# A graph layer and an expert layer on one core: statistics of the nodes with three reciprocal roots, and another order of bias transfers, turns and the last sum

## The reference, cut to what matters

```
x [6250, 256] f32; src, dst [100000] int32 (edges sorted by dst)
def mlp(h): return relu(h @ w1 + b1) @ w2 + b2

xn   = layernorm(x)
msgs = mlp(xn[dst])                          # one message an edge
agg  = segment_sum(msgs, src, 6250)          # summed by source node
x    = x + mlp(xn + agg)

f = layernorm(x)                             # one "batch" of 6250 tokens
w = softmax(softmax(mean(f) @ Wr + br) * capacity scale); top 2 of 8 experts
y = sum over the 2 experts: w_e * (gelu(f @ W1[e] + b1[e]) @ W2[e] + b2[e])
out = x + layernorm(y + f) * gamma + beta
```

## Time and profile before

| | before |
|---|---|
| runs | 1018.24, 1019.18 (median), 1019.61 us |
| profiled execution | 1018.42 us |
| its span, first to last instruction | 1016.6 us |
| busy: PE, DVE, POOL, ACT | 91%, 77%, 60%, 56% |
| granted TensorE clock, mean | 0.964 |

### The profile page before, as it was taken

One profiled execution on the slowest core, in us unless ns is written; L12 is line 12 of the kernel. 1 busy time (PEld: TensorE's weight loads), 2 busy tenths in 40 slices (PEclk: granted clock), 3 DMA queues, 4 the chain that ended last, 5 costly groups with the idle time before them and its releaser, 6 DMA issues.

```text
span 1016.6 us, 15925 instructions
## 1 busy us (share of the span) xinstructions
PE 925.1 (91%) x5067; PEld 549.2 (54%) x5067; DVE 784.3 (77%) x2245; ACT 569.3 (56%) x1143; POOL 609.9 (60%) x635
## 2 busy tenths in 40 slices
PE   5899994869999999899999999999489999999996
PEld 2455552334555555555555555555256666766675
DVE  7889993986776776866876876865668788889995
ACT  6899962435355354455454455454278677566661
POOL 2102114767777777777777777777005667666774
PEclk8899897999999999999999999999769999999999
DMA  9853899333433443434334434333120000000001
GB/s 302 118 100 99 143 143 306 109 84 97 139 102 105 112 122 101 113 104 133 102 98 115 121 98 125 105 98 105 27 94 6 22 22 22 33 32 21 22 22 63
DMA packets 61740, 98.66 MB, mean 97 GB/s; under 512 B 9014, under 2 KB 47399, under 8 KB 61655
## 3 DMA queue, kind: packets, MB, share of 16 engines
q0 software_dynamic: 26640, 61.37, 25.1%
q1 hardware_dynamic: 34426, 35.31, 10.9%
q10 hardware_dynamic: 588, 0.93, 0.3%
HBM read 77.79 MB, written 19.78 MB: 96 GB/s over the span
## 4 chain that ended last, share of the span: by engine, by line
PE 66%; DVE 14%; ACT 8%; issue 4%; DMA 4%; POOL 3%; SPq 0%; DVEq 0%; ACTq 0%; POOLq 0%
PE bank L1325 23%; PE bank L1473 12%; PE bank L1459 11%; PE bank L1315 6%; PE bank L1306 6%; PE bank L1345 3%; DMA zb_table<-G 2%; POOL G L799 2%; PE bank L1200 2%; DVE G L1908 1%; PE bank L1215 1%; ACT XT L950 1%; PE bank L1355 1%; DVE G L1906 1%; ACT G L992 1%
## 5 line engine op out<-in xcount | busy, mean ns | idle before, releaser
L865 POOL DMA_INDIRECT G<-table,edge_row x355 | 354.6, 999 | 113.9 <-issue 107.2
L1325 PE MATMUL bank<-G,MHL 128*128 128x512 f16 x1372 | 353.0, 380 | 0.2 <-DVE XT L1937 0.2
L1010 ACT ACTIVATE G<-bank 128x512 f16<-128x512 f32 x343 | 203.8, 597 | 215.5 <-PE bank L1315 214.6
L1325 PEld LDWEIGHTS bank<-G,MHL 128*128 128x128 f16 x1372 | 132.6, 97 | 96.0 <-issue 1.6
L1315 PE MATMUL bank<-G 128*128 128x256 f16 x686 | 135.1, 278 | 12.7 <-DVE G L1908 12.5
L1908 DVE TENSOR_TENSOR G<-iota_two,in_cell 128x512 f16<-128x512 f16 x343 | 144.1, 420 | 0.0
L1906 DVE TENSOR_TENSOR G<-iota_two,in_cell 128x256 f16<-128x256 f16 x343 | 99.6, 290 | 43.9 <-PE bank L1315 19.0
L1473 PE MATMUL bank<-MHL 128*128 128x256 f16 (+1 forms) x1176 | 130.6, 273 | 0.4 <-DVE G L2179 0.3
L1473 PEld LDWEIGHTS bank<-MHL 128*128 128x128 f16 (+1 forms) x1176 | 115.2, 98 | 16.6 <-DVE MHL L2023 0.7
L1315 PEld LDWEIGHTS bank<-G 128*128 128x128 f16 x686 | 66.1, 98 | 95.6 <-DVE G L1908 20.2
L1459 PE MATMUL bank<-G,MHL 128*128 128x512 f16 x528 | 115.9, 379 | 1.9 <-ACT G L1082 1.9
(11 more groups left out here) (345 smaller groups left out, 1234.1 us busy)
## 6 DMA issues: line engine op xcount, KB each, us to landing
X<-in_L_gnn_b POOLq DMA_DIRECT2D x12, 512.0 KB, 12.9
zb_table<-G SPq DMA_DIRECT2D x12, 512.0 KB, 4.7
table<-MHL SPq DMA_DIRECT2D x12, 512.0 KB, 6.2
XT<-zb_table SPq DMA_DIRECT2D x12, 512.0 KB, 3.9
G<-table,edge_row POOLq DMA_INDIRECT x355
out<-G SPq DMA_DIRECT2D x11, 512.0 KB, 2.9
X<-in_x SPq DMA_DIRECT2D x2, 1536.0 KB, 14.8
X<-in_x SPq DMA_DIRECT2D x2, 1024.0 KB, 10.6
```

What stands on the lines that cost most here:

```text
L865: e.indirect_dma_start(rows[g % RING][:, j, :], None, table, bass.IndirectOffsetOnAxis(ap=edge_row[:, at:at + 1], axis=0),).then_inc(s_row ...
L1010: e.activation(blocks[c % ARING].rearrange("p a b -> p (a b)")[:, 0:n], bank[3 + c % 2][:, 0:n], ACT.Copy).then_inc(s_ev, 1)
L1325: ins = e.matmul(bank[1 + m][:, :], MHL[:, t, h * D + m * P:h * D + (m + 1) * P], blocks[c % ARING].rearrange("p a b -> p (a b)"), start=( ...
```

## The change

There are six parts.

1. **Statistics.** The batches of tiles are cut a little otherwise, and the reciprocal roots are taken apart from them: `scale_tiles(j)` makes one root for each range of `STAT_ROOTS`, three in all instead of six. The first two batches stand ahead of the keys, the next behind the first sorting stage with the bounds, and the last behind the second stage.
2. **Jobs in the sort.** `copy_low(0)` to `copy_low(9)` stood ahead of stages 8, 13, 17, 20, 24, 30, 35, 42, 48 and 53 and stand now behind stages 2, 6, 11, 15, 17, 23, 29, 35, 41 and 47. `copy_low(10)`, which stood behind the sort, stands behind stage 54 of 55. TensorE's three small jobs go one step later.
3. **First nodes.** `transposes(0)` goes ahead of the second product of the bound, and ACT counts 1 and then, behind `copy_turned(0)`, 3 instead of 4 at once.
4. **Bias transfers.** POOL issues eight of them ahead of the run list instead of five, and the run list and the load of `run_first` then directly one after the other.
5. **The tail.** `root_slot` and `turn_slot` replace the fixed distances for the last items: tiles 24, 25 are turned in slot 133 instead of 131, tiles 26, 27 in slot 136 instead of 132; tile 47 gets its root in slot 136 instead of 132 and its turn in 138 instead of 134. The one-hots of the last sum are made one slot sooner, ahead of the roots of tiles 24 to 27.
6. **ACT's copy of a round** stands at the head of its slot instead of at its end.

```diff
 Y_BANKS = 3
-STAT_BATCHES = [(0, 4), (4, 8), (8, 16), (16, 28), (28, 40), (40, TILES)]
+STAT_BATCHES = [(0, 4), (4, 8), (8, 16), (16, 28), (28, 38), (38, TILES)]
+STAT_ROOTS = [(0, 8), (8, 16), (16, TILES)]
 STAT_MOST = max(z - a for a, z in STAT_BATCHES)
...
         SLOTS_ALL = items[-1][0] + TURN_AFTER + 1
+        LAST_SUM = PRE + 2 * (GROUPS * ROUNDS - 1)
         ITEM_TILES = [len(tiles) for _, tiles in items]
...
+        def root_slot(s):
+            t, tiles = items[s]
+            return LAST_SUM + 3 if tiles[0] == TILES - 2 else t + ROOT_AFTER
+        def turn_slot(s):
+            t, tiles = items[s]
+            if tiles[0] == TILES - 2:
+                return LAST_SUM + 5
+            at = t + TURN_AFTER
+            if at == LAST_SUM - 1:
+                return LAST_SUM + 3
+            return LAST_SUM if at == LAST_SUM - 2 else at
+        def turns_due(k):
+            return [(s, tiles) for s, (_, tiles) in enumerate(items) if turn_slot(s) == k]
         def roots_due(k):
             out = []
-            for s, tiles in due(k, ROOT_AFTER):
+            for s, tiles in ((s, tiles) for s, (_, tiles) in enumerate(items) if root_slot(s) == k):
                 if tiles[0] >= FIRST:
...
-            for q in range(5):
+            for q in range(8):
                 add_b2(q)
             e.wait_ge(s_run_at, 2)
             e.dma_start(run_list.rearrange("(p t) -> p t", t=A_STRIDE), runs_t[0:n_class, :]).then_inc(s_run_list, 16)
-            add_b2(5)
             e.wait_ge(s_run_list, 16)
             e.indirect_dma_start(run_first[0:CLASS_ROWS, :], None, run_list.rearrange("(r t) -> r t", t=1),
                                  bass.IndirectOffsetOnAxis(ap=class_run[0:CLASS_ROWS, 0:1], axis=0)).then_inc(s_run_first, 16)
-            for q in range(6, STEPS):
+            for q in range(8, STEPS):
                 add_b2(q)
...
                 for i, t in enumerate(tiles_of(q)):
-                    e.wait_ge(s_stat, 1 + sum(t >= z for _, z in STAT_BATCHES))
+                    e.wait_ge(s_stat, 1 + sum(t >= z for _, z in STAT_ROOTS))
                     e.activation(xn_in[q % 2][:, i, :], X[:, t, :], ACT.Identity, bias=nmr[:, t:t + 1],
...
                              bias=abs_b1[:, m:m + 1], scale=LNORM_MAX).then_inc(s_hbc, 1)
-            count_more(4)
+            count_more(1)
...
             copy_turned(0)
+            count_more(3)
             normalise(1)
...
                 copy_blocks([c + 2 for c in chunks_of(k) if c + 2 < CHUNKS])
-                for s, tiles in due(k, TURN_AFTER):
+                for r in round_due(k, 0):
+                    if r == 0:
+                        e.wait_ge(s_keep, 1)
+                    e.wait_ge(s_agg, GROUPS * (r + 1))
+                    since(e, s_tu, max(r - 1, 0))
+                    e.activation(U[r % 2][:, :], bank[0][:, 0:D], ACT.Copy, scale=keep[:, 0:1]).then_inc(s_uh, 1)
+                for s, tiles in turns_due(k):
                     e.wait_ge(s_tx, s + 1)
...
                         e.activation(h, h, ACT.Relu).then_inc(s_hd, 1)
-                for r in round_due(k, 0):
-                    if r == 0:
-                        e.wait_ge(s_keep, 1)
-                    e.wait_ge(s_agg, GROUPS * (r + 1))
-                    since(e, s_tu, max(r - 1, 0))
-                    e.activation(U[r % 2][:, :], bank[0][:, 0:D], ACT.Copy, scale=keep[:, 0:1]).then_inc(s_uh, 1)
             e.wait_ge(s_dif, 1)
...
             ins.then_inc(s_hb, 1)
-            e.wait_ge(s_hbc, KD)
-            for k in range(KD):
-                e.matmul(bank[7][0:1, 0:D], hidden_bound[:, k:k + 1], abs_w[1][:, k, :], start=(k == 0), stop=False)
-            e.matmul(bank[7][0:1, 0:D], ones[0:1, 0:1], abs_b2[0:1, :], start=False, stop=True).then_inc(s_hb, 1)
-
             def transposes(q):
...
                     ins.then_inc(s_tp, 1)
+            transposes(0)
+            e.wait_ge(s_hbc, KD)
+            for k in range(KD):
+                e.matmul(bank[7][0:1, 0:D], hidden_bound[:, k:k + 1], abs_w[1][:, k, :], start=(k == 0), stop=False)
+            e.matmul(bank[7][0:1, 0:D], ones[0:1, 0:1], abs_b2[0:1, :], start=False, stop=True).then_inc(s_hb, 1)
...
-            transposes(0)
             e.wait_ge(s_scale, 1)
             e.matmul(bank[7][:, 0:2], ones[0:1, :], bound[0:1, 2:4], start=True, stop=True).then_inc(s_scp, 1)
             for q in range(STEPS):
                 hidden(q)
                 if q + 1 < STEPS:
                     transposes(q + 1)
-                if q == 3:
+                if q == 4:
                     rank_rows()
-                elif q == 4:
+                elif q == 5:
                     sum_runs()
-                elif q == 5:
+                elif q == 6:
                     turn_runs()
...
                     multiply(c)
-                for s, tiles in due(k, TURN_AFTER):
+                for s, tiles in turns_due(k):
                     turn_x(s, tiles)
...
                     step(e.bn_aggr(mv2[:, t, :], stat_in[:, t - a, :]))
+            def scale_tiles(j):
+                a, z = STAT_ROOTS[j]
                 settle()
...
-            aux = {1: [(statistics, 1), (scale_bounds,), (statistics, 2)], 6: [(statistics, 3)], 7: [(copy_low, 0)],
-                   11: [(row_tiles,)], 12: [(copy_low, 1)], 14: [(class_numbers,)],
-                   16: [(class_counts,), (copy_low, 2), (select_rows,)], 18: [(class_runs,)],
-                   19: [(statistics, 4), (copy_low, 3)], 23: [(copy_low, 4)], 25: [(class_rows_of,)], 28: [(statistics, 5)],
-                   29: [(copy_low, 5)], 34: [(copy_low, 6), (run_starts,)], 41: [(copy_low, 7)],
-                   47: [(copy_low, 8), (place_rows,)], 52: [(copy_low, 9)]}
+            aux = {1: [(statistics, 2), (scale_bounds,), (scale_tiles, 1), (statistics, 3), (statistics, 4)],
+                   2: [(statistics, 5), (scale_tiles, 2), (copy_low, 0)], 6: [(copy_low, 1), (row_tiles,)],
+                   11: [(copy_low, 2)], 14: [(class_numbers,)], 15: [(copy_low, 3)],
+                   16: [(class_counts,), (select_rows,)], 17: [(copy_low, 4)], 18: [(class_runs,)],
+                   23: [(copy_low, 5)], 25: [(class_rows_of,)], 29: [(copy_low, 6)],
+                   34: [(run_starts,)], 35: [(copy_low, 7)], 41: [(copy_low, 8)],
+                   47: [(copy_low, 9), (place_rows,)], 54: [(copy_low, 10)]}
             s_, d_ = src_in[0:EDGE_ROWS, :], dst_in[0:EDGE_ROWS, :]
...
             statistics(0)
+            statistics(1)
+            scale_tiles(0)
             e.wait_ge(s_dst, 16 * len(EDGE_PARTS))
...
             sum_flags()
-            copy_low(10)
             copy_low(11)
...
-                if slot(k)[0] == "gather":
+                if slot(k)[0] == "gather" and k < LAST_SUM:
                     one_hots(*slot(k)[1:])
...
                 prepare(k + 2)
+                if k + 3 == LAST_SUM:
+                    one_hots(*slot(k + 3)[1:])
                 if k + 2 < BATCHES:
```

## The result

| | before | changed |
|---|---|---|
| median of 20 runs each | 1019.09 us | 1016.14 us |
| lowest and highest | 1016.72, 1021.70 us | 1013.06, 1019.09 us |
| ratio, 95% interval | | 0.9972 (0.9963 to 0.9980) |
| span of the profiled execution | 1016.6 us | 1014.3 us |
| busy: PE, DVE, POOL, ACT | 91%, 77%, 60%, 56% | 91%, 77%, 60%, 56% |

By the ratio the changed kernel is 0.28% faster, 2.9 us. The forecast was 4.0 us faster, 1015.2 us.

A forecast was written before the change was run, and what follows sets the result against it. TensorE's products were taken as the bound except in the sorting phase and the tail of the sums. -1.4 (sorting) - 2.6 (tail) = -4.0 us on 1018.42 gave 1014.4, forecast as 1015.2 for the median; range 1010.5 to 1020.5.

The forecast's parts named there:

- The start, +1.5: Start of the sorting phase: statistics moved ahead make `scale_bounds`, and ACT's loop with it, 1.5 us later.
- Rival 2: Sorting phase: the sort is not late, as TensorE's clock rises earlier or ACT gains; 2.6 us more, 1012.6; chance 0.12.
- The end of the sort, 157.2: Sorting phase: early low-half copies wait for ACT, so the key list goes out at 157.2 instead of 149.24 us.
- The relief: Sorting phase: bias additions end before the sort does, so ACT's 2.35 and 6.60 us store waits go and later landings shrink.
- the mark: End of the sorting phase, when POOL may issue the third class batch: 179.3 instead of 180.71 us, a gain of 1.4.
- rival 1: After the sort: landings stay as long while the sort ends later, 1024.6 us; chance 0.25 including a half relief.
- The tail, -2.6: Last sums: one-hots ahead of the root and tile 47's root behind DVE's addition bring that addition 2.6 us sooner.
- The middle, 0: Middle phase: ACT's copy leading its slot for each round was costed at nothing.
- Rival 4: Sorting phase: TensorE falls to 1.2 GHz once more, costing ACT one to three us, 1017; chance 0.13 together with another rival.

The follow-up runs named there:

- third run of the changed kernel: The changed kernel with nothing further edited, timed again against the kernel before on one chip: 1015.96 against 1022.54 us, ratio 0.9936.

## Why the prediction was right, and where not

**The start, +1.5.** Right: `scale_bounds` came 1.49 us later (25.18 to 26.67). ACT's loop ran 1.2 us later in the trace of the result (its first copy into `G` at 36.23 instead of 35.05), because TensorE's first hidden products, which begin at 28.49 instead of 27.03, took 6.06 us instead of 6.35: they began 1.5 us later, and the granted clock rose less than that later (0.68 and 0.90 in 32 to 34), so fewer of them ran at 1.2 GHz. How much that gives differs from trace to trace. In the third run of the changed kernel the same products took 5.08 us, and ACT's copy began at 35.36, only 0.4 us later than with bias order and tail (34.97, on another chip). Rival 2 named this; it gave 0.3 us in one trace and more than a microsecond in the other.

**The end of the sort, 157.2.** Right: 156.70, with `copy_low(8)` at 132.99 (133.4 forecast) and `copy_low(10)` in time. DVE waits for ACT's high copies as forecast.

**The relief, and the mark 179.3.** The mark is 179.28. Its terms: key list at 156.70 (forecast 157.2), 3.92 to the first windows (4.6), 15.77 to the merge (14.6), 2.89 to the batch (2.9). That the mark is met to the tenth is luck: the first two terms were 1.2 us too long together, and the third, whose class windows took about 6 us to land instead of 3.5 to 4.8, was 1.2 us too short. The runs show more than this sum said: the relief does not need the later sort (mark 173.00 with the bias order alone), and without the relief the change is slower than before (mark 191.11).

**The reason for the relief** was left undecided, and rival 1 drew the wrong conclusion from a right rule. The prediction set the rule of the Trainium skill (DMA: Bandwidth & Descriptors, "Queues, rings and completion order": engines take turns between queues at packet level) against the 24.4 us store, and said that by this rule the backlog would not be the cause. The packets of the queues agree with the rule, and show why the backlog is a cause all the same. DMA view of the kernel before, 106 to 150 us, in each microsecond of which both queues moved packets (packets, MB, share of 16 engines):

```profile
q0 software_dynamic: 3034, 3.02, 69.1%
q1 hardware_dynamic: 3005, 2.98, 25.0%
```

and its part from 125 to 135 us:

```profile
q0 software_dynamic: 691, 0.68, 80.0%
q1 hardware_dynamic: 690, 0.69, 25.3%
```

and with the bias order alone, same stretch:

```profile
q0 software_dynamic: 514, 0.51, 55.4%
q1 hardware_dynamic: 1056, 1.05, 31.8%
```

Before, POOL's queue (q0) and SP's (q1) moved 3034 and 3005 packets, and 691 and 690: one for one, as that rule of the Trainium skill has it. A packet of the accumulating bias addition took 0.185 us here on average (80.0% of 160 engine-microseconds over 691), one of a store 0.059 us. The better measure is what a queue moves alone: with the bias order alone, additions moved 408 packets in 112 to 117 us, 82 a microsecond, and stores 682 packets in 119 to 121 us, 341 a microsecond. SP has two stores a step, 1056 packets every 10.4 us, and while POOL's queue always has something, only 690 get through in 10 us. So the stores fall behind step by step. With an addition that ends in its step (9.2 us), the stores have the rest of the engines' time and all 1056 get through. What a backlog takes away is mainly the pauses in which the stores catch up; a store's packet itself took 0.059 instead of 0.048 us. Rival 1 was argued from this rule and fell with the runs, the rule didn't.

One thing in the traces doesn't fit equal turns. In the changed kernel SP issued a store at 119.09, while POOL's two additions were moving, and not one of its packets moved before 124.80; POOL's queue moved 455 packets meanwhile. Before, the store issued at 97.09 moved its first packet at 102.70, behind 433. So such a store first waits over five microseconds, and then takes turns. Why is open.

**The tail, -2.6.** Right in mechanism: DVE's addition for the round followed the statistics of tile 47 directly, and the root fitted behind it (DVE still waited 0.56 us for TensorE's product). Its size is less sure than the numbers look. The pair of traces gives 3.05 at the addition and 3.2 at the column sum, the timed run of the tail alone 2.5 (0.9 to 4.0). But the old tail takes 16.54 us in one trace, its products partly at 1.2 GHz, and 14.50 in another, and the new one 12.3 to 13.4.

**The middle, 0.** This is the step that failed: "costed at nothing" was wrong by 2.4 us in this trace, though not through ACT's copy. Two falls of TensorE's clock behind pauses that were there before took nearly all of it. Rival 4 had the mechanism, but looked for it in the sorting phase only. With them -1.3 (first gather) - 3.2 + 2.4 is -2.1, against -2.9 by the ratio; without them it would have been -4.5, and the forecast -4.0. That the measured time came within a microsecond of the forecast is in part luck, then: the clock took in the middle what the tail gave beyond its 2.6, and more.

**What the forecast did not ask** is which part earns the time. The whole gain and more is in the bias order and the tail (0.9892); what was done to the sort costs some of it back. The estimate of the later sort was on paper (the key list at 157.2 instead of 149.24, 8 us), and the relief that it was "paid with" was summed with it, while the bias order gives the relief without the later sort (mark 173.00).

## What to carry to other kernels

When a change has parts that move a mark both ways, price each part alone before taking their sum for the change: here one hunk of POOL's order gives 9.6 us, and the statistics, roots and job table beside it take back about 5 at the first gather (4 to 8 by the ratios). A queue of slow packets (accumulating DMAs) should be fed one at a time in step with the loop, since a burst of them takes every second turn from the stores beside it. Early statistics, early copies and the other engine's step rate hang together: with the copies moved back and the statistics left early, TensorE and DVE waited elsewhere. And a gain of two or three microseconds read from one pair of traces should be checked against the granted clock of both: the last sum before ran partly at 0.50 in one trace of the old tail and at 1.00 in the other.

## What the runs showed of the hardware that was not expected

- Alone, accumulating additions of 512 KB moved 82 packets of about 1 KB a microsecond and plain stores 341 (bias order alone, 112 to 117 and 119 to 121 us). Side by side with a backlog, both queues get the same number of packets: 3034 and 3005 in 106 to 150 us of the kernel before, 2901 and 2844 with the tail alone.
- A store issued at the start of a backlog of additions moved no packet for over five microseconds (119.09 to 124.80 us in the changed kernel, 109.31 to 114.79 in the change without the bias order, 97.09 to 102.70 before); 433 to 455 packets of POOL's queue went first.
- With the DMA engines full, the way from the key list's issue to the mark took 31.5 us in one trace and 34.0 in another with the same program up to there, store landing in 24.4 and 27.6 us. With the engines free it took 24.5 to 24.9 us in five traces on three chips.
- Pauses of TensorE of 2.2 and 3.6 us in an otherwise full phase are followed by 1.2 GHz in some programs and not in others, and again in the same places when the changed kernel was run again: 0.9 and 1.4 us a time.
